# Attention: narrow products in column and row tiles, and the decay's bias added by VectorE

## The chip, the core and the metric

The kernel runs on 1 core of one Trainium2 chip. The metric is the device time of one execution in microseconds (us), lower is better. Times shown are of whole executions; the profile is of one of them.

## What is computed

A layer of two halves. The first is an RWKV-6 attention over x of shape (2, 4096, 512), behind a layer norm with a learned shift and scale; the second a feed-forward part with 4-bit block quantization. The change touches the attention alone. Cut to what matters there:

```
sx  = shift(x) - x
xxx = x + sx * time_maa_x
m   = tanh(xxx @ tm_w1).reshape(B, T, 5, 32)          # tm_w1: 512 x 160
mix = time_maa_wkvrg + einsum('btfa,fac->btfc', m, tm_w2)
xw, xk, xv, xr, xg = [x + sx * mix[:, :, i] for i in range(5)]
r, k, v, g = xr @ Wr, xk @ Wk, xv @ Wv, silu(xg @ Wg)
ww  = time_decay + tanh(xw @ td_w1) @ td_w2           # td_w1: 512 x 64, td_w2: 64 x 512
w   = exp(-exp(ww))
# per head, over time: y_t = r_t (state + u k_t v_t'); state = w_t * state + k_t v_t'
out = groupnorm(y) * g @ Wo
```

## The kernel before

Tokens go in 32 blocks of 128 per sequence, both sequences (B = 2) together, so that a block has BT = 256 columns; channels lie on the 128 partitions in G = 4 groups. `attention` writes each engine's order out by hand: `pe_body`, `act_body`, `dve_body`, `pool_body` and `sp_body` are called for i = 0 to 33 and work in one pass on three blocks. Block i is mixed and projected (`do_p`), block i - 1 goes through the recurrence (`do_w`), block i - 2 through the output product (`do_f`). Most passes run in a hardware loop of three laps with nine passes written out in each. Engines meet at semaphores, one `Signal` each; `after(engine, signal, block, k)` is a wait.

In a pass TensorE first does eight steps of 32 tokens for the recurrence: `pe_scores` (L404, L408, L410, L415, matmuls in 32x32 tiles) and `pe_y` (L430, L433, likewise). Between the steps stand the two halves of `pe_g` (L509), `pe_td1` (L474), the five mixing products `pe_delta` (L462), two output products `pe_wo` (L522, 512 columns) and `pe_td2` (L482). Then come the k, r and v projections `pe_proj` (L495), with `pe_x` (L442, transposes of the next block) and `pe_tm1` (L450) among them.

The places that the change touches:

- `pe_tm1` multiplies `xxx` by `tm_w1`: its first 128 columns give mixings 0 to 3, with one 128x128 stationary tile per channel group; its last 32 give mixing 4, with a 128x32 tile and all 256 token columns. Both write to `SMALL`, one PSUM bank.
- `act_m` (L575 to L578) takes the tanh of both, once as fp32 and once rounded to fp32r; `dve_m` (L752, L753) forms the rest, the difference of the two.
- `act_stack` (L588) copies, for each mixing, the 32 rows of value or rest into four partition groups of `m_stack`, 20 copies a block. `act_affine` (L604) follows on ScalarE; VectorE's `dve_z` (L918) waits for it.
- `pe_td1` multiplies the mixed `xf` by `td_w1` into 64 rows of `SMALL`; ScalarE's tanh (L671) writes `u1`, whose 65th row holds ones. `pe_td2` multiplies by `w_td2`, whose 65th row is the decay bias, into the two banks `PROJ`. `dve_ww` (L774) takes the minimum with 80 into `wexp`, and ScalarE's two exponentials (L616, L619) follow.
- VectorE's steps are `dve_A` (L865, L872, L878, L894), one per recurrence step, and `dve_mix` (L762), one per mixing. A mixing waits for its product and frees `PROJ` for the next.

Of the kernel before, what the change touches and what calls it, by code (L numbers as in the profile page):

```python
# [30 lines left out]
ALU = mybir.AluOpType  # L31
ACT = mybir.ActivationFunctionType
AX_X = mybir.AxisListType.X

HEADS = [slice(r, r + 32) for r in range(0, 128, 32)]
E_MAX = 1e30

P = 128
B, T, C = 2, 4096, 512
H, K = 16, 32  # L40
G = C // P
HG = P // K
A_RANK, D_RANK = 32, 64
NMIX = 5
TC = 128
NI = T // TC
BT = B * TC
Q = TC // 32
NX = G * B * Q
EPS = 1e-5  # L50
# [40 lines left out]
def after(eng, signal, chunk, k=None):  # L91

    value = signal.at(chunk, k)
    if not isinstance(value, int) or value > 0:
        eng.wait_ge(signal.sem, value)
# [40 lines left out]
def attention(nc, x1, x, maa_x, maa, tm_w1, tm_w2, decay, td_w1, td_w2, faaaa, Wr, Wk, Wv, Wg, Wo,  # L136
              ln_w, ln_b, c_in, wmod, ident_in, diag_in, pick_in, ni=NI):
    with ExitStack() as ctx:
        ctx.enter_context(nc.allow_non_contiguous_dma(reason="per-channel columns, a few hundred bytes each"))

        def sb(name, shape, dt=F32):
            return ctx.enter_context(nc.sbuf_tensor(name, shape, dt))
# [14 lines left out]
        w_tm1 = sb("w_tm1", [P, G, NMIX * A_RANK])  # L157
        w_tm2 = sb("w_tm2", [P, NMIX, C], F32R)
        w_td1 = sb("w_td1", [P, G, D_RANK])
        w_td2 = sb("w_td2", [D_RANK + 1, C])  # L160

        col_maax, col_u = sb("col_maax", [P, G]), sb("col_u", [P, G])
        col_maa = sb("col_maa", [P, NMIX, G])
        col_sa, col_ca = sb("col_sa", [P, G, B]), sb("col_ca", [P, G, B])
        col_lnw, col_lnb = sb("col_lnw", [P, G]), sb("col_lnb", [P, G])
# [13 lines left out]
        m_full = xxx[:, 0:2].rearrange("p g b t -> p g (b t)")  # L179
        m_hi = xxx[:, 2:4].rearrange("p g b t -> p g (b t)")  # L180
        m_part = (m_hi.bitcast(F32R), m_full.bitcast(F32R))
        u1 = sb("u1", [D_RANK + 1, BT])
        rT = sb("rT", [P, G, B, TC])
        kvar = sb("kvar", [P, 4, G, B, TC])
        rcol = sb("rcol", [P, NX, SEND])
# [39 lines left out]
        with nc.Block() as blk:  # L225
            @blk.sync
            def _(sp):
                def load(dst, src):
                    sp.dma_start(dst, src).then_inc(loaded, 16)
                    n_loads[0] += 1  # L230
                sp.dma_start(kvar[:, 0:2].rearrange("p a g b t -> p (a g b t)").rearrange("p (g n) -> p g n", g=G),
                             wmod[:, 0:C].rearrange("(g p) n -> p g n", p=P)).then_inc(mod_loaded, 16)
                sp.dma_start(kvar[:, 2:4].rearrange("p a g b t -> p (a g b t)").rearrange("p (g n) -> p g n", g=G),
                             wmod[:, C:2 * C].rearrange("(g p) n -> p g n", p=P)).then_inc(mod_loaded, 16)
                sp.dma_start(rcol_flat[:, 0:G * C].rearrange("p (g n) -> p g n", g=G),
                             wmod[:, 2 * C:3 * C].rearrange("(g p) n -> p g n", p=P)).then_inc(mod_loaded, 16)
                for g in range(G):
                    sp.dma_start(c_t[:, g, :], c_in[:, g * P:(g + 1) * P].rearrange("b p -> p b")).then_inc(mod_loaded, 16)
                for dst, src in ((w_r[:], Wr), (w_k[:], Wk), (w_v[:], Wv), (w_g[:], Wg), (w_o_raw, Wo), (w_tm1[:], tm_w1), (w_td1[:], td_w1)):
                    load(dst, src.rearrange("(g p) n -> p g n", p=P))  # L240
                for part in range(4):
                    load(w_full[A_RANK * part:A_RANK * (part + 1)], tm_w2.rearrange("f a n -> a f n"))
                load(w_td2[0:D_RANK, :], td_w2)
                load(ident[:], ident_in)
                load(diag[:], diag_in)
                load(pick_f, pick_in)
                load(col_maax[:], maa_x.rearrange("(g p) -> p g", p=P))
                load(w_td2[D_RANK:D_RANK + 1, :], decay.unsqueeze(0))
                load(col_u[:], faaaa.rearrange("(g h) k -> (h k) g", g=G))
                for f in range(NMIX):  # L250
                    load(col_maa[:, f, :], maa[f].rearrange("(g p) -> p g", p=P))
                load(col_lnw[:], ln_w.rearrange("(g p) -> p g", p=P))
                load(col_lnb[:], ln_b.rearrange("(g p) -> p g", p=P))
                sp.wait_ge(loaded, 16 * n_loads[0])

            @blk.gpsimd
            def _(pool):
                nc.gpsimd.memset(neg_half[:], -0.5)
                nc.gpsimd.memset(state[:], 0.0)
                nc.gpsimd.memset(u1[:], 1.0)  # L260
                nc.gpsimd.memset(F4[:], 1.0)
                nc.gpsimd.memset(G4[:], 1.0).then_inc(zeroed, 1)

# [181 lines left out]
        def pe_tm1(pe, i):  # L445
            after(pe, xxx_done, i)
            after(pe, hT_done, i)
            for lo, hi, o in ((0, P, 0), (P, NMIX * A_RANK, BT)):
                for k in range(G):
                    last = nc.tensor.matmul(SMALL[0:hi - lo, o:o + BT], w_tm1[:, k, lo:hi],  # L450
                                            xxx[:, k].rearrange("p b t -> p (b t)"), start=(k == 0), stop=(k == G - 1))
            last.then_inc(tm1_done.sem, 1)

        def pe_delta(pe, i, j):
# [14 lines left out]
        def pe_td1(pe, i):  # L469
            xf_wait(pe, i, 0)  # L470
            after(pe, mf_done, i)
            after(pe, gu_done, i - 1)
            for k in range(G):
                last = nc.tensor.matmul(SMALL[0:D_RANK, 0:BT], w_td1[:, k, :], xf[:, 0, k].rearrange("p b t -> p (b t)"),  # L474
                                        start=(k == 0), stop=(k == G - 1))
            last.then_inc(td1_done.sem, 1)

        def pe_td2(pe, i):
            after(pe, u1_done, i)
            after(pe, mixed, i)  # L480
            for g in range(G):
                last = nc.tensor.matmul(PROJ[g // 2][:, (g % 2) * BT:(g % 2 + 1) * BT], w_td2[:, g * P:(g + 1) * P], u1[:],  # L482
                                        start=True, stop=True)
            last.then_inc(td2_done.sem, 1)

        def pe_proj(pe, i, j, free, halves=(0, 1)):
# [86 lines left out]
        def act_m(act, i):  # L573
            after(act, tm1_done, i)
            nc.scalar.activation(m_full[:, 0], SMALL[:, 0:BT], ACT.Tanh)  # L575
            nc.scalar.activation(m_full[0:A_RANK, 1], SMALL[0:A_RANK, BT:2 * BT], ACT.Tanh)
            nc.scalar.activation(m_part[0][:, 0], SMALL[:, 0:BT], ACT.Tanh)
            nc.scalar.activation(m_part[0][0:A_RANK, 1], SMALL[0:A_RANK, BT:2 * BT], ACT.Tanh).then_inc(mf_done.sem, 1)  # L578

        def act_stack(act, i):  # L580
            after(act, mf_done, i)
            after(act, m_done, i)
            after(act, delta_done, i - 1)
            for j in range(NMIX):
                f = ORDER[j]
                src = slice(A_RANK * (f % 4), A_RANK * (f % 4 + 1))
                for part in range(4):
                    last = nc.scalar.activation(m_stack[A_RANK * part:A_RANK * (part + 1), j, :], m_part[part % 2][src, f // 4, :], ACT.Copy)  # L588
                last.then_inc(m_stacked.sem, 1)

        def act_yT(act, c, b):
# [71 lines left out]
        def act_body(act, i, do_p, do_w, do_f, more, more2):  # L663
            c, f = i - 1, i - 2
            if do_w:
                act_gu(act, c, 0)
                act_gu(act, c, 1)
            if do_p:
                after(act, td1_done, i)
                after(act, td2_done, c)  # L670
                nc.scalar.activation(u1[0:D_RANK, :], SMALL[0:D_RANK, 0:BT], ACT.Tanh).then_inc(u1_done.sem, 1)  # L671
            if more:
                act_xn(act, i + 1)
            if do_w:
                act_yT(act, c, 0)
            if do_p:
                act_w(act, i)
            if do_p:
                act_fg(act, i)
                act_k(act, i, 0)  # L680
            if do_w:
                act_yT(act, c, 1)
            if more:
                act_hT(act, i + 1)
            if do_w:
                act_square(act, c)
            if do_p:
                act_k(act, i, 1)
                act_r(act, i, 0)
                act_r(act, i, 1)  # L690
                act_k32(act, i)
                act_m1(act, i)
            if more:
                act_m(act, i + 1)
            if more:
                act_stack(act, i + 1)
            if do_w:
                act_affine(act, c)
# [51 lines left out]
        def dve_m(dve, i):  # L750
            after(dve, mf_done, i)
            nc.vector.tensor_tensor(m_part[1][:, 0], m_full[:, 0], m_hi[:, 0], ALU.subtract)  # L752
            nc.vector.tensor_tensor(m_part[1][0:A_RANK, 1], m_full[0:A_RANK, 1], m_hi[0:A_RANK, 1], ALU.subtract).then_inc(m_done.sem, 1)  # L753

        def dve_mix(dve, i, j):
            after(dve, delta_done, i, j + 1)
# [13 lines left out]
        def dve_ww(dve, i):  # L770

            after(dve, td2_done, i)
            after(dve, m_stacked, i)
            nc.vector.tensor_scalar(flat4(wexp), banks[:, 2:4].rearrange("p s n -> p (s n)"), 80.0, None, ALU.min).then_inc(ww_done.sem, 1)  # L774

        def dve_der_w(dve, i):

# [922 lines left out]
```

## Time and profile before

| | us |
|---|---|
| median of 3 runs | 4545.55 |
| lowest and highest | 4528.36 and 4548.22 |
| the profiled execution | 4564.24 |
| its span, first to last instruction | 4562.4 |
| TensorE busy in it | 3895.7 (85%) |
| VectorE busy | 3591.5 (79%) |
| ScalarE busy | 1506.1 (33%) |
| GpSimd busy | 1182.1 (26%) |

PE is TensorE's matmuls and PEld its weight loads, which overlap; DVE is VectorE, ACT ScalarE, POOL GpSimd. A fp32 matmul shows as two records, a fp32r one as one. "Issue" is idle time in which an engine waited for nothing that the profile shows. L numbers are lines of the kernel before.

### The profile page before, as it was taken

What the parts mean: (1) busy time and instruction counts of PE and PEld (TensorE: products, weight loads), DVE (VectorE), ACT (ScalarE), POOL (GpSimd) and SP (SyncE); (2) the same over time, 40 slices, a digit from 0 to 9 for tenths busy, and PEclk for the clock granted to TensorE, in tenths of its full rate; (3) what the DMA queues carried; (4) which work ended last, traced back from release to release, by engine and by line L of the source; (5) the groups of instructions that cost most, each with busy time, mean ns of one, the idle gap of its engine ahead of it and who ended that gap; (6) DMA issues with size and microseconds to landing.
All of it is one profiled execution on the core that took longest, in us unless ns stands there. A gap on an engine that the chain in (4) does not pass through costs nothing. (4 is left out here: it accounts for less than half of the span.)

```text
span 4562.4 us, 152511 instructions
## 1 busy us (share of the span) xinstructions
PE 3895.7 (85%) x64712; PEld 2623.4 (57%) x64712; DVE 3591.5 (79%) x7929; ACT 1506.1 (33%) x2683; POOL 1182.1 (26%) x736
## 2 busy tenths in 40 slices
PE   4889888888988888898898942499999999999998
PEld 3767676666766766777676721244444444444444
DVE  4777877867776776777787739789999999999997
ACT  2434343343433433434342302233333232323232
POOL 1121211112111121212212104433333333333332
PEclk7999998989999999999998965699999999999999
DMA  3000000000000000000000020000101111010100
GB/s 106 12 27 21 22 26 19 29 17 22 26 22 22 21 22 26 22 26 17 26 21 17 21 92 28 14 29 29 36 28 36 31 33 34 30 36 29 36 28 29
DMA packets 72983, 133.01 MB, mean 29 GB/s; under 512 B 12705, under 2 KB 13473, under 8 KB 72290
## 3 DMA queue, kind: packets, MB, share of 16 engines
q1 hardware_dynamic: 72290, 123.00, 8.5%
q8 instruction: 528, 8.65, 0.8%
q14 instruction: 165, 1.35, 0.1%
HBM read 89.43 MB, written 33.55 MB: 27 GB/s over the span
## 5 line engine op out<-in xcount | busy, mean ns | idle before, releaser
L712 POOL TENSOR_TENSOR xf<-xf,hT 128x1024 f32<-128x1024 f32 x128 | 309.3, 2417 | 1209.1 <-DVE xf L762 1209.1
L878 DVE COPY_PREDICATED Am<-pick,banks 128x64 f32<-128x64 uint8 (+2 forms) x1792 | 460.5, 257 | 125.4 <-DVE Am L878 8.6
L1580 PE MATMUL fbank<-gT,xqT 128*128 128x464 f16 (+1 forms) x2304 | 492.0, 364 | 61.6 <-ACT xqT L1503 60.0
L1602 PE MATMUL fbank<-dT,hqT 128*128 128x512 f16 x2112 | 488.4, 380 | 50.7 <-ACT hqT L1513 50.7
L1580 PE MATMUL fbank<-uT,xqT 128*128 128x464 f16 (+1 forms) x2304 | 488.2, 362 | 2.1 <-issue 2.1
L1527 ACT ACTIVATE sil<-fbank,und 128x464 f32<-128x464 f32 (+1 forms) x192 | 125.1, 652 | 860.4 <-PE fbank L1580 860.4
L723 POOL TENSOR_TENSOR yrs<-yvar,neg_half 128x32 f32<-128x32 f32 x32 | 174.0, 5437 | 896.3 <-DVE yvar L907 896.3
L1580 PEld LDWEIGHTS fbank<-gT,xqT 128*128 128x128 f16 x2304 | 221.2, 98 | 313.0 <-issue 84.6
L1580 PEld LDWEIGHTS fbank<-uT,xqT 128*128 128x128 f16 x2304 | 225.3, 98 | 234.8 <-issue 5.5
L1602 PEld LDWEIGHTS fbank<-dT,hqT 128*128 128x128 f16 x2112 | 196.9, 98 | 266.1 <-issue 33.4
L762 DVE SCALAR_TENSOR_TENSOR xf<-banks,col_maa,sx 128x256 f32<-128x256 f32 x640 | 265.2, 477 | 94.8 <-PE banks L462 94.3
L522 PE MATMUL banks<-w_o,yn 128*128 128x512 f32 x512 | 293.6, 727 | 19.8 <-DVE yn L918 15.9
L1385 POOL TENSOR_TENSOR hq<-q16h,s16h 128x1408 f16<-128x1408 f16 x64 | 163.7, 2558 | 523.9 <-DVE hq L1338 523.9
L588 ACT ACTIVATE m_stack<-xxx 32x256 fp32r<-32x256 f32 x640 | 264.9, 414 | 75.9 <-DVE xxx L753 58.9
L509 PE MATMUL banks<-xf,w_g 128*128 128x256 f32 x1024 | 260.9, 411 | 7.3 <-issue 4.0
L430 PE MATMUL banks<-Am,v_s 32*32 32x32 f32 x8192 | 192.6, 198 | 85.1 <-issue 79.2
L865 DVE TENSOR_TENSOR Am<-banks,diag 128x128 f32<-128x128 f32 x256 | 72.5, 283 | 238.7 <-PE banks L415 233.7
L495 PE MATMUL banks<-xf,w_k 128*128 128x256 f32 x1024 | 249.2, 398 | 7.5 <-issue 6.1
L433 PE MATMUL banks<-r,state 32*32 32x32 f32 x8192 | 192.3, 196 | 52.1 <-issue 52.1
L430 PEld LDWEIGHTS banks<-Am,v_s 32*32 32x32 f32 x8192 | 160.5, 108 | 127.9 <-issue 123.0
L495 PE MATMUL banks<-xf,w_v 128*128 128x256 f32 x1024 | 229.5, 382 | 0.0
L509 PEld LDWEIGHTS banks<-xf,w_g 128*128 128x128 f32 x1024 | 204.5, 205 | 41.8 <-issue 5.7
(233 smaller groups left out, 8417.5 us busy)
## 6 DMA issues: line engine op xcount, KB each, us to landing
x_tok<-in_L_attn_x SPq DMA_DIRECT2D x32, 512.0 KB, 4.0
xres<-in_L_attn_x SPq DMA_DIRECT2D x32, 512.0 KB, 3.6
x_after_attention<-xres SPq DMA_DIRECT2D x32, 512.0 KB, 3.7
xl<-x_after_attention SPq DMA_DIRECT2D x64, 256.0 KB, 2.8
xr<-x_after_attention SPq DMA_DIRECT2D x64, 256.0 KB, 2.8
out<-xr SPq DMA_DIRECT2D x64, 256.0 KB, 2.1
raw_g<-in_L_wmod SPq DMA_DIRECT2D x3, 1024.0 KB, 5.1
raw_g<-in_L_ffn_w_gate SPq DMA_DIRECT2D x1, 2816.0 KB, 11.4
```

What stands on the lines that cost most here:

```text
L430: nc.tensor.matmul(out, v_s[d, g, b, q, :], Am[d, n % 2, g, :], start=True, stop=False)
L433: last = nc.tensor.matmul(out, state[d, b, q, g, :], r32[d, X, :], start=False, stop=True)
L495: last = nc.tensor.matmul(PROJ[h][:, (g % 2) * BT:(g % 2 + 1) * BT], w[:, k, g * P:(g + 1) * P], buf[:, k].rearrange("p b t -> p (b t)"), ...
L509: last = nc.tensor.matmul(SMALL[:, (g % 2) * BT:(g % 2 + 1) * BT], w_g[:, k, g * P:(g + 1) * P], xf[:, NMIX - 1, k].rearrange("p b t -> p ...
L522: last = nc.tensor.matmul(SMALL[:], yn[:, k, b, :], w_o[:, b, k, :], start=(k == 0), stop=(k == G - 1))
L588: last = nc.scalar.activation(m_stack[A_RANK * part:A_RANK * (part + 1), j, :], m_part[part % 2][src, f // 4, :], ACT.Copy)
L712: nc.gpsimd.tensor_tensor(xf[:, j % NXF].rearrange("p g b t -> p (g b) t"), xf[:, j % NXF].rearrange("p g b t -> p (g b) t"), hT[:, :, :, ...
L723: nc.gpsimd.tensor_tensor(yrs[:], yvar[:], neg_half[:], ALU.pow).then_inc(yrs_done.sem, 1)
L762: last = nc.vector.scalar_tensor_tensor(xf[:, j % NXF, g], PROJ[g // 2][:, (g % 2) * BT:(g % 2 + 1) * BT].rearrange("p (b t) -> p b t", b= ...
L878: nc.vector.copy_predicated(dst, mask, src).then_inc((done or A_step).sem, 1)
L1580: last = nc.tensor.matmul(GU[2 * pair + t][:, 0:w], xqT[:, u, a, g, :], W[:, b_, g, lo_:hi_], start=(k == 0), stop=(k == 3 * G - 1))
L1602: last = nc.tensor.matmul(DN[1 - u][:], hqT[:, a, kk, :], dT[:, b_, kk, :], start=(k == 0), stop=(k == 3 * KF - 1))
```

## The change

Three things change in the attention.

The last 32 columns of `tm_w1`: the 256 token columns are cut in four runs of QT = 64, and each run goes to its own column tile (32 stationary columns, output on partitions 0, 32, 64, 96). So the result lies as 128 rows of 64 columns, not as 32 rows of 256. Tanh and difference run on that shape, and the copies for mixing 4 bring each run back to its columns: sixteen copies of 64 columns instead of four of 256.

The decay's first product runs as two column tiles of 64, one per sequence; its second as two row tiles, each with its own half of `u1`, its own copy of `w_td2` and its own bank. `PROJ[b]` now holds one sequence; before, each bank held two channel groups of both.

The bias row and the row of ones go. The bias is loaded as the column `col_decay`, and VectorE adds it in `dve_ww`, in four instructions, one for each channel group. The memset of `u1` goes, `td_w2` is loaded twice.

```
-        w_td2 = sb("w_td2", [D_RANK + 1, C])
+        w_td2 = sb("w_td2", [P, C])
+        col_decay = sb("col_decay", [P, G])
-        u1 = sb("u1", [D_RANK + 1, BT])
+        u1 = sb("u1", [P, TC])
...
-                load(w_td2[0:D_RANK, :], td_w2)
+                for b in range(B):
+                    load(w_td2[HALVES[b], :], td_w2)
-                load(w_td2[D_RANK:D_RANK + 1, :], decay.unsqueeze(0))
+                load(col_decay[:], decay.rearrange("(g p) -> p g", p=P))
...
-                nc.gpsimd.memset(u1[:], 1.0)
...
-            for lo, hi, o in ((0, P, 0), (P, NMIX * A_RANK, BT)):
-                for k in range(G):
-                    last = nc.tensor.matmul(SMALL[0:hi - lo, o:o + BT], w_tm1[:, k, lo:hi],
-                                            xxx[:, k].rearrange("p b t -> p (b t)"), start=(k == 0), stop=(k == G - 1))
+            for k in range(G):
+                nc.tensor.matmul(SMALL[:, 0:BT], w_tm1[:, k, 0:P], xxx[:, k].rearrange("p b t -> p (b t)"), start=(k == 0), stop=(k == G - 1))
+            for k in range(G):
+                for d, rows in enumerate(HEADS):
+                    last = nc.tensor.matmul(SMALL[rows, BT:BT + QT], w_tm1[:, k, P:P + A_RANK], xxx[:, k].rearrange("p b t -> p (b t)")[:, QT * d:QT * (d + 1)],
+                                            start=(k == 0), stop=(k == G - 1))
...
             for k in range(G):
-                last = nc.tensor.matmul(SMALL[0:D_RANK, 0:BT], w_td1[:, k, :], xf[:, 0, k].rearrange("p b t -> p (b t)"),
-                                        start=(k == 0), stop=(k == G - 1))
+                for b in range(B):
+                    last = nc.tensor.matmul(SMALL[HALVES[b], 0:TC], w_td1[:, k, :], xf[:, 0, k, b], start=(k == 0), stop=(k == G - 1))
...
-            after(pe, u1_done, i)
-            after(pe, mixed, i)
+            settled_after(pe, mod_done, (u1_done, i), (mixed, i))
             for g in range(G):
-                last = nc.tensor.matmul(PROJ[g // 2][:, (g % 2) * BT:(g % 2 + 1) * BT], w_td2[:, g * P:(g + 1) * P], u1[:],
-                                        start=True, stop=True)
+                for b in range(B):
+                    last = nc.tensor.matmul(PROJ[b][:, g * TC:(g + 1) * TC], w_td2[HALVES[b], g * P:(g + 1) * P], u1[HALVES[b]], start=True, stop=True)
...
-            nc.scalar.activation(m_full[0:A_RANK, 1], SMALL[0:A_RANK, BT:2 * BT], ACT.Tanh)
+            nc.scalar.activation(m_full[:, 1, 0:QT], SMALL[:, BT:BT + QT], ACT.Tanh)
...
-                    last = nc.scalar.activation(m_stack[A_RANK * part:A_RANK * (part + 1), j, :], m_part[part % 2][src, f // 4, :], ACT.Copy)
+                    rows = HEADS[part]
+                    if f < 4:
+                        last = nc.scalar.activation(m_stack[rows, j, :], m_part[part % 2][HEADS[f], 0, :], ACT.Copy)
+                    else:
+                        for d in range(4):
+                            last = nc.scalar.activation(m_stack[rows, j, QT * d:QT * (d + 1)], m_part[part % 2][HEADS[d], 1, 0:QT], ACT.Copy)
...
-                nc.scalar.activation(u1[0:D_RANK, :], SMALL[0:D_RANK, 0:BT], ACT.Tanh).then_inc(u1_done.sem, 1)
+                nc.scalar.activation(u1[:], SMALL[:, 0:TC], ACT.Tanh).then_inc(u1_done.sem, 1)
...
-            nc.vector.tensor_tensor(m_part[1][0:A_RANK, 1], m_full[0:A_RANK, 1], m_hi[0:A_RANK, 1], ALU.subtract).then_inc(m_done.sem, 1)
+            nc.vector.tensor_tensor(m_part[1][:, 1, 0:QT], m_full[:, 1, 0:QT], m_hi[:, 1, 0:QT], ALU.subtract).then_inc(m_done.sem, 1)
...
-            nc.vector.tensor_scalar(flat4(wexp), banks[:, 2:4].rearrange("p s n -> p (s n)"), 80.0, None, ALU.min).then_inc(ww_done.sem, 1)
+            for g in range(G):
+                last = nc.vector.tensor_scalar(wexp[:, g], banks[:, 2:4, g * TC:(g + 1) * TC], col_decay[:, g:g + 1], 80.0, ALU.add, ALU.min)
+            last.then_inc(ww_done.sem, 1)
```

`HEADS` are the four runs of 32 partitions, `HALVES` the two of 64.

TensorE's order of the first pass, around the three products (each row: line, operation, output and inputs, output's shape, count of matmuls). Before:

```order
L450 MATMUL banks<-xxx,w_tm 128x256 x4
L450 MATMUL banks<-xxx,w_tm 32x256 x4
L462 MATMUL banks<-m_stack,w_tm 128x256 x8
L474 MATMUL banks<-xf,w_td 64x256 x4
L462 MATMUL banks<-m_stack,w_tm 128x256 x12
L482 MATMUL banks<-u,w_td 128x256 x4
```

With the change:

```order
L451 MATMUL banks<-xxx,w_tm 128x256 x4
L454 MATMUL banks<-xxx,w_tm 32x64 x16
L466 MATMUL banks<-m_stack,w_tm 128x256 x8
L479 MATMUL banks<-xf,w_td 64x128 x8
L466 MATMUL banks<-m_stack,w_tm 128x256 x12
L486 MATMUL banks<-u,w_td 128x128 x8
```

Nothing has changed places; 12 matmuls a block have become 32, and each streams fewer columns.

ScalarE's order from the tanh of the mixings to the gate's, with the change:

```order
L578 ACTIVATE xxx<-banks 128x256
L579 ACTIVATE xxx<-banks 128x64
L580 ACTIVATE xxx<-banks 128x256
L581 ACTIVATE xxx<-banks 128x64
L592 ACTIVATE m_stack<-xxx 32x256 x16
L595 ACTIVATE m_stack<-xxx 32x64 x16
```

Before, the last two rows were one, twenty copies of 32x256.

## Rows read from the trace of the kernel before

**Rows 1.** The page: span and busy shares.
```profile
span 4562.4 us, 152511 instructions
...
PE 3895.7 (85%) x64712; PEld 2623.4 (57%) x64712; DVE 3591.5 (79%) x7929; ACT 1506.1 (33%) x2683; POOL 1182.1 (26%) x736
```

**Rows 2.** Windows: us, then busy (count) of PE, PEld, DVE, ACT, POOL, granted clock, DMA.
```profile
500.00:1000.00 500.00, 444.44 (x10567) 349.68 (x10567) 376.91 (x936) 187.93 (x398) 97.22 (x43) 0.92 0.08 24
```

**Rows 3.** Waits of PE, 100 to 2600 us: waiting, releaser: total, times, longest.
```profile
PE banks L430 <- issue: 77.0, 50, 2.5
...
PE banks L415 <- DVE kT L852: 23.1, 31, 0.7
```

**Rows 4.** Waits of DVE, 100 to 2600 us.
```profile
DVE Am L865 <- PE banks L415: 205.0, 68, 6.3
...
DVE xf L762 <- PE banks L462: 88.7, 66, 4.2
DVE xxx L774 <- PE banks L482: 35.8, 21, 3.9
```

**Rows 5.** Groups of PE, 100 to 2600 us: form xrecords | busy, mean ns | idle before.
```profile
L482 PE MATMUL banks<-u,w_td 65*128 65x256 f32 x252 | 106.3, 594 | 2.7 <-DVE xf L762 2.7
L474 PE MATMUL banks<-xf,w_td 128*64 128x256 f32 x248 | 68.8, 427 | 0.0
L450 PE MATMUL banks<-xxx,w_tm 128*32 128x256 f32 x248 | 59.3, 382 | 0.0
```

**Rows 6.** Timeline of PE: start, length, line, records, idle before.
```profile
1199.78 3.37 PE L474 MATMUL banks<-xf,w_td 128*64 128x256 f32 x8
...
1210.13 0.76 PE L404 MATMUL banks<-rcol,kvar 32*32 32x80 f32 x32
...
1210.80 0.23 PE L410 MATMUL banks<-rcol,kvar 32*32 32x16 f32 x8
...
1212.72 0.22 PE L430 MATMUL banks<-Am,v_s 32*32 32x32 f32 x3 [0.65 <-issue]
...
1216.12 0.20 PE L410 MATMUL banks<-rcol,kvar 32*32 32x16 f32 x1 [1.01 <-issue]
```

**Rows 7.** Timeline of PE later: tm1 and a second td1.
```profile
1245.78 3.73 PE L450 MATMUL banks<-xxx,w_tm 128*128 128x256 f32 x16
...
1278.41 1.94 PE L474 MATMUL banks<-xf,w_td 128*64 128x256 f32 x8
```

**Rows 8.** DMA queues, 100 to 2600 us: packets, MB, share.
```profile
q8 instruction: 429, 7.03, 1.2%
```

**Rows 9.** Windows: a stretch and the one right after it.
```profile
1195.90:1199.30 3.40, 1.67 (x159) 1.53 (x148) 3.26 (x9) 0.00 (x0) 2.09 (x1) 1.00 0.02 5
1199.30:1202.70 3.40, 3.29 (x23) 1.97 (x24) 2.46 (x12) 0.00 (x0) 0.98 (x3) 0.50 0.03 7
```

**Rows 10.** Timeline of ACT in one block.
```profile
1250.36 0.36 ACT L578 ACTIVATE xxx<-banks 32x256 fp32r<-32x256 f32 x1
1252.88 8.55 ACT L588 ACTIVATE m_stack<-xxx 32x256 fp32r<-32x256 f32 x20 [2.15 <-DVE xxx L753]
1261.45 2.07 ACT L604 ACTIVATE yn<-yn,col_lnb,col_lnw 128x256 f32<-128x256 f32 x4
```

**Rows 11.** Timeline of DVE in one block.
```profile
1229.54 0.29 DVE L865 TENSOR_TENSOR Am<-banks,diag 128x128 f32<-128x128 f32 x1 [4.77 <-PE banks L415]
...
1266.11 1.25 DVE L918 TENSOR_TENSOR yn<-yn,gate 128x1024 f32<-128x1024 f32 x1
1269.68 1.66 DVE L762 SCALAR_TENSOR_TENSOR xf<-banks,col_maa,sx 128x256 f32<-128x256 f32 x4 [2.33 <-PE banks L462]
```

**Rows 12.** Groups of ACT, 100 to 2600 us.
```profile
L616 ACT ACTIVATE xxx<-xxx 128x1024 f32<-128x1024 f32 x32 | 33.8, 1056 | 574.4 <-DVE xxx L774 574.4
...
L564 ACT ACTIVATE hT<-hT 128x8 f32<-128x8 f32 x31 | 6.7, 217 | 1.9 <-PE banks L442 0.4
```

**Rows 13.** Timeline of DVE in the set-up.
```profile
42.63 0.21 DVE L285 CAST pick<-yT 128x112 uint8<-128x112 f32 x1
```

More of the change, by code:

```diff
@@ L47 @@
 BT = B * TC
+QT = BT // 4
+HALVES = [slice(0, 64), slice(64, 128)]
 Q = TC // 32
@@ L159, in attention @@
         w_td1 = sb("w_td1", [P, G, D_RANK])
-        w_td2 = sb("w_td2", [D_RANK + 1, C])
-        col_maax, col_u = sb("col_maax", [P, G]), sb("col_u", [P, G])
+        w_td2 = sb("w_td2", [P, C])
+        col_maax, col_u, col_decay = sb("col_maax", [P, G]), sb("col_u", [P, G]), sb("col_decay", [P, G])
         col_maa = sb("col_maa", [P, NMIX, G])
@@ L575, in act_m @@
             nc.scalar.activation(m_full[:, 0], SMALL[:, 0:BT], ACT.Tanh)
-            nc.scalar.activation(m_full[0:A_RANK, 1], SMALL[0:A_RANK, BT:2 * BT], ACT.Tanh)
+            nc.scalar.activation(m_full[:, 1, 0:QT], SMALL[:, BT:BT + QT], ACT.Tanh)
             nc.scalar.activation(m_part[0][:, 0], SMALL[:, 0:BT], ACT.Tanh)
-            nc.scalar.activation(m_part[0][0:A_RANK, 1], SMALL[0:A_RANK, BT:2 * BT], ACT.Tanh).then_inc(mf_done.sem, 1)
+            nc.scalar.activation(m_part[0][:, 1, 0:QT], SMALL[:, BT:BT + QT], ACT.Tanh).then_inc(mf_done.sem, 1)
         def act_stack(act, i):
@@ L585, in act_stack @@
                 f = ORDER[j]
-                src = slice(A_RANK * (f % 4), A_RANK * (f % 4 + 1))
                 for part in range(4):
-                    last = nc.scalar.activation(m_stack[A_RANK * part:A_RANK * (part + 1), j, :], m_part[part % 2][src, f // 4, :], ACT.Copy)
+                    rows = HEADS[part]
[4 more added lines that the diff above has]
+                            last = nc.scalar.activation(m_stack[rows, j, QT * d:QT * (d + 1)], m_part[part % 2][HEADS[d], 1, 0:QT], ACT.Copy)
                 last.then_inc(m_stacked.sem, 1)
```

## The prediction

> **What bounds the kernel now.** Read the busy shares first [rows 1]: no engine is at its limit over the whole span. The change touches the attention stage alone, some 2,500 us of it, so I go to windows inside it [rows 2]: TensorE is busy 444.44 of 500 us, VectorE 376.91, ScalarE 187.93, at a granted clock of 0.92. Then the waits. TensorE hardly waits for anyone: for VectorE's transpose of k 23.1 us in all [rows 3]. Its other idle time is "issue", the largest entry 77.0 us in 50 places, though the program holds no wait there. VectorE does wait, and for TensorE: 205.0 us for scores, 88.7 for the mixing's products, 35.8 for the decay's [rows 4]. So the end of this stage is set by TensorE's own chain: its matmuls, its issue stalls, and its clock. ScalarE and VectorE matter where their slack is small.
>
> The decay's first product ran 248 records, 8 per block of tokens, so 31 blocks in 2,500 us: 80.6 us a block [rows 5]. The sum is made per block and multiplied by 32.
>
> **TensorE's matmuls.** All three products are fp32, each matmul two records. td2 takes 106.3 us over 252 records, 3.37 a block; td1 68.8 over 248, 2.22; tm1's narrow half 59.3 over 248, 1.91 [rows 5]. tm1's sixteen records take 3.73 us [rows 7], its narrow half, with 32 stationary columns, 1.91 of it: array columns left idle cost full time. After the change td1 and td2 stream 128 columns per matmul in two tiles, tm1's rest 64 in four. Do tiles run side by side? 32 records of 80 columns in 32x32 tiles take 0.76 us [rows 6]; at the pace of a 256-column record (3.73 us for 16, 0.23 each [rows 7]) one by one they would take 32 x 0.073 = 2.3 us. So tiles that share neither rows nor columns overlap fourfold, less the last one's drain. Tiles that share rows (td1, tm1) are not in the trace. Bounds: no gain, or the full factor. I take the full factor, since the 32x32 rows are the nearest. td2 halves, -1.69; td1 halves, -1.11; tm1's rest goes to a quarter, -1.43. Together -4.23 us a block.
>
> A rule speaks against tm1's part, whose factor is taken from the moving columns. The Trainium skill, TensorEngine Tiling (Array Packing), section Performance Considerations, gives each matmul an overhead of about 60 cycles and warns against dividing a dimension that is already small. At 2.4 GHz an estimate by it is 25 ns x 32 records = 0.8 us where I have 0.48, some 10 us less gain in all. The trace disagrees: eight 16-column records end within 0.23 us [rows 6].
>
> **Instruction supply.** 429 instruction packets of 16 KB fed TensorE in this stretch [rows 8], 13.8 a block, about 250 instructions each. The stalls at 1212.72 and 1216.12 lie 3.40 us apart, and the records from the one to the other are 45, 4 for a mixing product and 78 for scores: 127 pairs of load and matmul, one packet [rows 6]. A packet of small matmuls is used up in about 2.4 us, yet the next comes only after 3.40. So a packet costs at least 3.4 us, and time saved inside a packet that takes less is lost. tm1 lies among 96 long projection records and td2 beside the output product: both keep their saving. td1 is surrounded by small tiles. With it at 1.94 us [rows 7] a packet holding it takes about 3.9, and after the saving 2.8, so 0.6 comes back as stall; at half clock (3.37 us [rows 6]) nothing does. I charge 0.55, with bounds 0 and 1.1. Besides, 20 more matmuls in the program are 80 instructions a block, 0.31 packet. TensorE's idle is 0.111 of 80.6 us, 9.0, less 0.75 for the transpose, over 13.8 packets 0.60 each: +0.19.
>
> **Clock.** Between 1195.9 and 1199.3 TensorE was busy 1.67 of 3.4 us, and the next stretch ran at 0.50, the 1.2 GHz level, although busy 3.29 of 3.40 [rows 9]. So low clock follows a stretch with little matmul work. The clock of 0.92 means some 13 us of low time a block. The change takes long work out of the small-tile stages, and I expect more such stretches. Each costs between 0 (small work follows) and 1.7 us (long work follows at half pace; td1 shows 3.37 against 1.94). I take one more every second block, +0.85, bounds 0 and 3.4 (two a block).
>
> **ScalarE.** For the last of the five mixings, four copies of 256 columns become sixteen of 64. Length by columns: 1,056 ns for 1,024, 217 for 8 [rows 12], 414 for 256 (20 in 8.55 us without overlap, [rows 10]), so about 0.20 us fixed and 0.84 ns a column: 0.25 for 64, 0.27 with the step. 16 x 0.27 less 4 x 0.43 is +2.6 us before the affine step; the shorter tanh and subtraction give back some 0.3. That lies on a path: the affine ends at 1263.52 and VectorE's gating product starts at 1266.11 [rows 10, 11], 2.6 of slack. tm1's saving moves VectorE 1.4 earlier, but the copies start hardly earlier, since they wait 2.15 us for VectorE's subtraction. The product is then late by up to 2.3 - 1.2 = 1.1. The next mixing waited 2.33 for TensorE in this block [rows 11], which hides it; where it doesn't wait, it counts. I charge 0.3, bounds 0 and 1.1.
>
> **VectorE.** ww becomes four instructions; the nearest row has four of 256 columns in 1.66 us [rows 11] where one took about 1.23, so 0 to +0.43. It is free: after it VectorE sat idle 4.77 us for the next scores [rows 11], behind the output product. Without that cover it would be 0.43. In the scores loop VectorE waits for TensorE at the scores and at 66 mixings only, of 155 [rows 4]; elsewhere it is itself the later one, and TensorE's saving is not passed on. I charge 0.6 of td1's and td2's, bounds 0 and 1.2.
>
> **Edits at no cost.** The second copy of the decay weights (128 KB) and the bias column hide behind VectorE's set-up, which reaches its first loaded operand at 42.63 with no idle before it [rows 13]. The dropped memset is on idle GpSimd. td2's waits are the same two, plus one long since met.
>
> **Sum.** -4.23 + 0.55 + 0.19 + 0.85 + 0.3 + 0.6 = -1.74 us a block, -56 in 32. Profiled execution: 4564.2 - 56 = 4508. The median of the runs, 4545.55, stands 18.7 below it, so I predict 4490 as a median.
>
> **Rivals.**
> 1. *Column tiles don't overlap*, as they share all rows: tm1 and td1 save nothing. Left are -1.69 + 0.19 + 0.4 (clock) + 0.3 = -0.8 a block, -26: about 4520. For: no row shows such tiles. Against: the 32x32 rows. Chance 0.12.
> 2. *Supply and clock take it all*: all of td1 lost, three more half-clock stretches every two blocks (2.55): -4.23 + 1.1 + 0.19 + 2.55 + 0.3 = -0.1, no change, 4540. For: issue stalls and low clock stand together in rows 6 and 9. The Trainium skill, TensorE: Matmul & The Clock Gate, section on why this matters, warns of throughput drops after idle gaps; rows 9 agree. Against: 2.8 us less of 46 is little. Chance 0.10.
> 3. *Slower: ScalarE's copies.* If 64 columns cost as much as 256 (0.43 a step), the copies grow by 5.2, the gating product comes 2.3 later than now, all of tm1's gain goes, and -4.23 + 1.43 + 2.3 + 0.55 + 0.19 + 0.85 = +1.1 a block, +35: 4580. It decides once a copy takes over 0.36. For: partition-shifted copies are only seen at 256. Against: the 8-column row of 217 ns. Chance 0.06.
> 4. *The tiles do nothing*, td2's included: about 4550. Chance 0.02.
>
> **How the numbers follow.** The forecast has 0.70: its own range, by the bounds, 4455 to 4520. With rivals 1 and part of 2 the range is 4455 to 4538. A measurement here tells about 0.5% (23 us) from no change. Faster: 0.70 and half of rival 1, 0.76. Same: the other half, rival 2, rival 4, 0.18. Slower 0.06.
>
> **What would show it.** td2's busy time near 53 us, td1's near 36, tm1's rest near 16; VectorE's wait for td2 (35.8) almost gone; more issue idle and a granted clock one or two hundredths lower in windows of this stage; copies of 64 columns near 0.25 us; the gating product waiting for the affine. Wrong if the copies take 0.4, if tm1's rest stays near 1.9 us a block, or if the clock falls below 0.89.

## The result, and the profile after

| | before | after |
|---|---|---|
| median of 4 runs each, us | 4545.99 | 4484.56 |
| lowest and highest | 4528.36, 4548.22 | 4470.44, 4490.96 |
| profiled execution | 4564.24 | 4490.96 |

The ratio is 0.9869, interval 0.9841 to 0.9897: faster by 1.3%. The forecast was 4490. The page of the kernel after, to set beside [rows 1]:

```profile
span 4488.8 us, 155551 instructions
...
PE 3793.4 (85%) x65992; PEld 2593.9 (58%) x65992; DVE 3589.2 (80%) x8025; ACT 1568.8 (35%) x3067; POOL 1181.0 (26%) x735
```

TensorE is busy 102 us less. How many of these the clock on the wall gets is best read from an instruction that comes once a block. VectorE's transpose of k, kernel before (durations in ns, then first and last start in us):

```profile
L852 DVE STREAM_TRANSPOSE kT<-kvar x32: 1201/1203/1204, 131.1 to 2622.5; 128x1024 f32<-128x1024 f32 x32
```

and after:

```profile
L861 DVE STREAM_TRANSPOSE kT<-kvar x32: 1201/1202/1204, 125.1 to 2558.5; 128x1024 f32<-128x1024 f32 x32
```

Over 31 intervals that is 80.37 us a block before and 78.50 after: -1.87, where the sum said -1.74. Of the 73 us between the two profiled executions 58 lie in these intervals, 6 ahead of the first transpose, 10 behind the last. By the windows of this stretch TensorE's busy time a block goes from 71.5 to 68.6 us, its idle time from 8.9 to 9.9. From here on "a block" means this spacing, and 2400 us of a window hold 2400 / 80.37 = 29.9 blocks before and 30.6 after.

The three products, groups of PE after, 100 to 2500 us (form, records, busy us, mean ns, idle before), beside [rows 5]:

```profile
L486 PE MATMUL banks<-u,w_td 64*128 64x128 f32 x480 | 55.7, 396 | 9.4 <-issue 6.7 <-DVE xf L769 2.7
L479 PE MATMUL banks<-xf,w_td 128*64 128x128 f32 x480 | 36.8, 293 | 8.9 <-issue 8.9
...
L454 PE MATMUL banks<-xxx,w_tm 128*32 128x64 f32 x992 | 20.3, 222 | 0.0
```

With 16, 16 and 32 records a block these are 1.86, 1.23 and 0.65 us, against 3.37, 2.22 and 1.91: -3.76 together. So tiles that share all their rows do run side by side. The mixing's product as a whole, timeline of PE, took 3.73 us [rows 7] and takes 2.5 now:

```profile
1210.58 1.89 PE L451 MATMUL banks<-xxx,w_tm 128*128 128x256 f32 x8
1212.39 0.65 PE L454 MATMUL banks<-xxx,w_tm 128*32 128x64 f32 x32
```

td1 is not always left whole. Here its sixteen records, 1.4 us in all, are cut by a stall that is longer than they are:

```profile
1240.46 0.43 PE L479 MATMUL banks<-xf,w_td 128*64 128x128 f32 x3
1242.68 0.93 PE L479 MATMUL banks<-xf,w_td 128*64 128x128 f32 x13 [1.79 <-issue]
```

Waits of PE after, 100 to 2500 us (total, times, longest), beside [rows 3]:

```profile
PE banks L432 <- issue: 62.7, 38, 3.3
...
PE banks L417 <- DVE kT L861: 23.1, 31, 0.7
...
PE banks L512 <- ACT gu L668: 12.5, 13, 1.7
PE banks L479 <- issue: 8.9, 6, 1.8
```

The issue entries of this view add up to 260.9 us in 197 places; before, in the same window, 230.3 in 170. Per block 7.71 became 8.53, +0.82. TensorE's wait for ScalarE at the gate's projection, 3.1 us before, is 12.5.

Waits of DVE after, 100 to 2500 us, beside [rows 4]:

```profile
DVE Am L874 <- PE banks L417: 189.2, 76, 5.3
DVE v_s L856 <- PE banks L498: 69.7, 31, 2.3
DVE xf L769 <- PE banks L466: 67.6, 65, 3.1
DVE yn L927 <- ACT yn L611: 24.7, 28, 1.7
...
DVE xxx L782 <- PE banks L486: 3.8, 6, 1.7
```

The wait for td2 (35.8) is all but gone. A new one is there: the gating product L927 waits for ScalarE's affine in 28 blocks, 0.8 us a block. Why, shows the timeline of ACT in one block:

```profile
1213.87 0.25 ACT L579 ACTIVATE xxx<-banks 128x64 f32<-128x64 f32 x1
...
1217.48 6.84 ACT L592 ACTIVATE m_stack<-xxx 32x256 fp32r<-32x256 f32 x16 [2.98 <-DVE xxx L760]
1224.34 4.23 ACT L595 ACTIVATE m_stack<-xxx 32x64 fp32r<-32x64 f32 x16
1228.60 2.08 ACT L611 ACTIVATE yn<-yn,col_lnb,col_lnw 128x256 f32<-128x256 f32 x4
1232.03 0.60 ACT L667 ACTIVATE gate<-banks 128x512 f32<-128x512 f32 x1 [1.35 <-DVE yn L927]
```

The copies take 11.1 us where they took 8.55 [rows 10], the affine ends that much later, the product with it, and the gate's eviction L667, which overwrites what the product reads, waits for the product. That is how TensorE comes to its 12.5 us. One row of windows, beside [rows 2], shows the clock, 0.91 for 0.92 (over 100 to 2500 us it is 0.93 in both kernels):

```profile
500.00:1000.00 500.00, 437.96 (x11127) 353.56 (x11129) 386.63 (x972) 209.26 (x500) 101.42 (x43) 0.91 0.07 22
```

### The profile page after: what moved, and what is told of

Read it like the earlier page. It is cut to its first block and busy times, and to the rows that moved or that the text cites. A ratio compares the mean times of both kernels' runs of the same rounds, so it can differ in the third digit from the quotient of the medians.

```text
span 4488.8 us, 155551 instructions
## 1 busy us (share of the span) xinstructions
PE 3793.4 (85%) x65992; PEld 2593.9 (58%) x65992; DVE 3589.2 (80%) x8025; ACT 1568.8 (35%) x3067; POOL 1181.0 (26%) x735
## 5 line engine op out<-in xcount | busy, mean ns | idle before, releaser
L512 PE MATMUL banks<-xf,w_g 128*128 128x256 f32 x1024 | 261.8, 413 | 14.1 <-ACT gu L668 12.5
L592 ACT ACTIVATE m_stack<-xxx 32x256 fp32r<-32x256 f32 x512 | 211.9, 414 | 99.6 <-DVE xxx L760 81.2
L623 ACT ACTIVATE xxx<-xxx 128x1024 f32<-128x1024 f32 x32 | 33.8, 1057 | 566.3 <-DVE xxx L782 566.3
```

What stands on the lines that cost most here:

```text
L512: last = nc.tensor.matmul(SMALL[:, (g % 2) * BT:(g % 2 + 1) * BT], w_g[:, k, g * P:(g + 1) * P], xf[:, NMIX - 1, k].rearrange("p b t -> p ...
L592: last = nc.scalar.activation(m_stack[rows, j, :], m_part[part % 2][HEADS[f], 0, :], ACT.Copy)
```

## The experiments

**How to read the ratios.** The runs came in three sets of four kernels, on chips where the kernel before took 4575.25, 4564.36 and 4551.42 us. So each kernel is told by its ratio to the kernel before on its own chip, with its 95% interval. 1% is 1.4 us a block. The change itself was timed only in the comparison above, against 4545.99 us, so where it is set beside one of these kernels, the two ratios come from different chips. And each kernel's trace is of one execution: a small difference between two traces is a hint and not a measurement.

### Each part alone

The first kernel is the kernel before with the mixing's narrow part of the change, its tanh, difference and copies; all else is as before.

```
+            for k in range(G):
+                for d, rows in enumerate(HEADS):
+                    last = nc.tensor.matmul(SMALL[rows, BT:BT + QT], w_tm1[:, k, P:P + A_RANK], ...[:, QT * d:QT * (d + 1)], ...)
```

> Only the narrow half of tm1 is tiled, with its sixteen copies; td1, td2 and the bias as before. Theory (ScalarE takes most of it): in the changed kernel's trace the place of tm1 shrank from 3.73 to 2.47 us, 1.26 a block, but the gating product waits 24.7 us in 30 blocks, 0.8 a block, for the affine behind the copies: net 0.3 to 0.6 a block, 10 to 20 us faster. Rival (the copies are hidden by mixing's waits for TensorE): all of 1.26 x 32, 40 us faster. Second rival (column tiles only pay together with the others): no change.

Measured 4514.14 us, ratio 0.9873 (0.9850 to 0.9896), 58 us faster, beyond even the rival's 40. That is 1.8 us a block (1.5 to 2.1 by the interval), more than the 1.26 that the product itself got shorter, although the price of the copies is paid in full. Waits of DVE, 100 to 2500 us:

```profile
DVE yn L926 <- ACT yn L612: 22.4, 27, 1.6
...
DVE xxx L782 <- PE banks L486: 14.0, 7, 3.9
```

The wait for the unchanged td2 fell from 31.2 us in this window to 14.0: a product that didn't change is waited for less. Something else had moved; what, this run doesn't tell.

The second has td1 as column tiles only; two tanh instead of one write both halves back to the old `u1`.

```
+                for b in range(B):
+                    last = nc.tensor.matmul(SMALL[HALVES[b], 0:TC], w_td1[:, k, :], xf[:, 0, k, b], ...)
```

> Only td1 runs in two column tiles; ScalarE brings the two halves back with two tanh. Theory (instruction supply takes half of what td1 saves): TensorE's place of td1 shrinks by 1.0 us a block, the issue idle in the scores steps near it grows by 0.3 to 0.6, so 10 to 20 us faster. Rival (supply takes nothing): 32 to 35 us faster. Rival (supply takes all): within 5 us of before.

Measured 4603.19, ratio 1.0067 (1.0040 to 1.0093): **slower**, by about 1 us a block, though td1 itself is 1 us shorter. All three expectations had it faster or the same. Group, wait and window of this kernel, 100 to 2500 us:

```profile
L477 PE MATMUL banks<-xf,w_td 128*64 128x128 f32 x464 | 37.1, 303 | 7.6 <-issue 7.6
```

```profile
PE banks L432 <- issue: 69.6, 35, 3.5
PE banks L435 <- issue: 68.5, 38, 2.5
```

```profile
100.00:2500.00 2400.00, 2103.24 (x50713) 1662.60 (x50713) 1738.82 (x4415) 876.24 (x1864) 459.86 (x202) 0.90 0.07 22
```

Its issue entries add up to 268.1 us in 29.3 blocks (82.0 us each), 9.2 a block, where the kernel before has 7.7 and the kernel with the bias alone, below, on the same chip, 8.1 (237.5 in 29.5 blocks): as much as td1 could save, or more. The granted clock is 0.90; those two have 0.93 and 0.92.

The third has td2 as row tiles with the bias on VectorE, and two tanh that fill the two halves of `u1`; the fourth has the bias alone.

```
+            for g in range(G):
+                last = nc.vector.tensor_scalar(wexp[:, g], PROJ[...], col_decay[:, g:g + 1], 80.0, ALU.add, ALU.min)
```

> td2 runs in two row tiles with its bias added by VectorE; td1 and tm1 as before, two tanh for u1. Theory (td2's saving passes whole, since VectorE waits for scores behind the output product right after it): 1.4 to 1.6 us a block, 45 to 50 us faster, the largest of the three parts. Rival (the wait moves to VectorE, whose chain of scores and mixings ends only then): 1.0 a block, about 30 us faster, and VectorE's wait before its next scores step grows instead of shrinking.

> Only the bias is moved: 64 rows in td2 without tiles, column added by VectorE in four instructions, no memset. Theory (hidden behind the output product): within 5 us of before, while the four instructions take 1.66 us in place of 1.23. Rival (they lie on the path): 0.43 x 32, 14 us slower.

Row tiles with the bias: 4508.52, ratio 0.9865 (0.9841 to 0.9888), 62 us faster where I had 45 to 50. The bias alone: 4584.18, ratio 1.0028 (1.0010 to 1.0046), 0.4 us a block, 13 us in all, which is the rival's price and not the theory's. So the four instructions, 1.66 us where one took 1.23, are not quite free. Against the bias alone the row tiles bring 1.6%, 2.3 us a block, for a product that got 1.6 us shorter (3.50 to 1.89). The granted clock over 100 to 2500 us is 0.94 in the one trace and 0.92 in the other; whether the rest of the gain came with it was not tested.

### Does the count of instructions cost?

20 small matmuls (80 instructions, as many as the change adds) into the kernel before, ahead of its wait for the transpose of k, on operands that are ready; what they write is overwritten. The same with 16 in the kernel with td1 alone.

```
             if n == 0:
+                for e in range(20):
+                    d = HEADS[e % 4]
+                    nc.tensor.matmul(scm[d, ...], kvar[d, 2, g, b, 32 * q:32 * q + 32], rcol[d, X, X0:SEND], start=True, stop=True)
```

> The kernel before with 20 more small matmuls a block: repeats of one 16-column score product, same values to the same place, put where TensorE waits 0.75 us for the transpose of k anyway. They bring as many instructions a block (80) as the change does and, hidden in that wait, no work on the path. Theory (where the packets of instructions begin within a block matters): the time moves by 15 us or more, either way, with TensorE's issue stalls standing at other places than before. Rival (only the amount of work matters): within 8 us of before.

> td1 alone in column tiles, which was 28 us slower than before, and now 16 of the same hidden small matmuls, so that the block has as many instructions as in the changed kernel. Theory (the loss of td1 alone came from the packets' places): 20 us or more faster than td1 alone. Rival (td1's saving is lost whatever the places, through stalls and a lower clock): the same as td1 alone within 10 us, ratio near 1.006.

Measured 4578.99, ratio 1.0052 (1.0026 to 1.0079), 0.7 us a block; and 4590.90, ratio 1.0060 (1.0038 to 1.0083), the same as td1 alone. So 80 more instructions cost 0.7 us where they hardly take room, above the 0.19 that I had charged; 64 more on top of td1 cost nothing that shows. How the 0.7 comes about is open. In the trace with 20 more TensorE's issue idle is 0.6 us a block above the kernel before (8.3 for 7.7), but its whole idle time is the same within 0.1 (9.0 for 8.9), since its waits for others are shorter; its busy time is 0.7 longer (72.2 for 71.5), of which the added products are some 0.3, and the granted clock is 0.91 for 0.93. The loss of td1 alone did not go away when its packets were shifted by 64 instructions; other shifts were not run.

### ScalarE's order

The affine is put ahead of the last mixing's copies, in the change and in the kernel before.

```
-                act_stack(act, i + 1)
+                act_stack(act, i + 1, range(NMIX - 1))
...
                 act_affine(act, c)
+            if more:
+                act_stack(act, i + 1, range(NMIX - 1, NMIX))
```

> The changed kernel with ScalarE's affine step moved ahead of the sixteen copies for the last mixing, which are needed only some 30 us later. Theory (the copies delay the gating product by 0.8 us a block): VectorE's wait for the affine (24.7 us) goes, 0.4 to 0.8 us a block, ratio 0.981 to 0.984 against 0.987 of the change. Rival (that wait only takes the place of the mixing's wait for TensorE): the wait goes, but the ratio stays 0.987.

> The same move of the affine step in the kernel before, where the gating product never waited for it. Both theories: within 8 us of before. It is the control for the run before this one, since here the instructions of TensorE are untouched: a change beyond 8 us would say that the time depends on small shifts that this study doesn't follow.

The change with it: 4478.21, ratio 0.9828 (0.9791 to 0.9864), the fastest kernel of all, though its interval overlaps that of the change. The kernel before with it: 4553.06, ratio 0.9974 (0.9950 to 0.9997), 11 us faster. That control was expected within 8 us, since no product waited for the affine there. So a move of this kind may bring 0.3% with no wait to remove, and the 0.4% in the change can't be put down to the affine on this evidence. Timelines of the change so ordered, first ACT, then DVE, in the block shown above:

```profile
1216.93 6.84 ACT L593 ACTIVATE m_stack<-xxx 32x256 fp32r<-32x256 f32 x16 [2.97 <-DVE xxx L763]
1223.91 2.08 ACT L612 ACTIVATE yn<-yn,col_lnb,col_lnw 128x256 f32<-128x256 f32 x4
```

```profile
1229.26 1.24 DVE L930 TENSOR_TENSOR yn<-yn,gate 128x1024 f32<-128x1024 f32 x1
```

The affine ends 9.1 us after the first copy begins (1216.93 to 1225.99) where it ended 13.2 after (1217.48 to 1230.68). The product no longer waits, and TensorE's wait at the gate's projection is 2.0 us where it was 12.5. The rival is right in part all the same. The next mixing now waits longer for TensorE:

```profile
DVE xf L772 <- PE banks L466: 86.8, 69, 3.9
```

That is 2.8 us a block where it was 2.2 (67.6 in the window), so of the 0.8 that VectorE no longer waits for the affine it waits 0.6 here.

### Leaving out one part

The change without td1's tiles, should the second experiment have shown td1 to be a loss, and the same with the affine moved; then the change without the mixing's part.

```
-                for b in range(B):
-                    last = nc.tensor.matmul(SMALL[HALVES[b], 0:TC], w_td1[:, k, :], xf[:, 0, k, b], ...)
+                last = nc.tensor.matmul(SMALL[0:D_RANK, 0:BT], w_td1[:, k, :], xf[:, 0, k].rearrange("p b t -> p (b t)"), ...)
```

> The changed kernel with td1 as it was before (one product of 256 columns), tm1 and td2 tiled. Theory (td1's tiles are a loss in company too, as alone: what they save comes back as issue stall and as half-clock time of the output product): faster than the change by about the 0.7% that td1 alone lost, ratio 0.978 to 0.983. Rival (the parts overlap, and td1's loss alone was of its own surroundings): ratio 0.987 to 0.993, the change or worse.

> The run before this one with the affine step moved ahead of the last mixing's copies. Theory: both gains add, ratio 0.974 to 0.979, the fastest of all. Rival (one takes the place of the other): 0.982 to 0.984, as with the moved affine alone.

> The changed kernel with tm1, its tanh and its copies as before: td1 and td2 alone. If parts add as they measured alone (td1 +0.7%, td2 -1.35%), ratio 0.993. If tm1's gain in company is only what its own place saves less the wait for the affine (0.4 a block, 15 us), then ratio 0.990. If tm1 gives nothing in company: 0.987.

| in the kernel | ratio to before | interval |
|---|---|---|
| tm1 | 0.9873 | 0.9850 to 0.9896 |
| td1 | 1.0067 | 1.0040 to 1.0093 |
| td2 and bias | 0.9865 | 0.9841 to 0.9888 |
| td1, td2 and bias | 0.9958 | 0.9940 to 0.9976 |
| tm1, td2 and bias | 1.0003 | 0.9983 to 1.0024 |
| the same, affine moved | 0.9914 | 0.9886 to 0.9941 |
| all (the change) | 0.9869 | 0.9841 to 0.9897 |

The change without td1's tiles took 4546.44 us, with the affine moved 4505.11, and without the mixing's part 4529.78. My expectation for the kernel without td1 fell, and the rival with it (0.987 to 0.993), as did both for the same with the affine moved (0.974 to 0.979, and 0.982 to 0.984). Two parts that each bring 1.3% bring nothing together, and td1, a loss by itself, brings 1.3% on top of them, if the change's ratio, from another chip, may be set beside theirs. Besides the tiles, the kernel without td1 has two tanh for `u1` where the change has one. td1 with td2 is near the product of the two (0.9931). The odd one is tm1 with td2: 2.6% short of 0.9740, 3.7 us a block.

Its trace shows something. Timeline of PE in five successive blocks, the rows that follow a stall in the first step's y products, between the output product and the k projection (and 1206.62, a stall in the last step before it):

```profile
1138.80 0.22 PE L435 MATMUL banks<-r,state 32*32 32x32 f32 x2 [1.99 <-issue]
...
1206.62 0.26 PE L432 MATMUL banks<-Am,v_s 32*32 32x32 f32 x2 [2.05 <-issue]
...
1217.80 0.26 PE L435 MATMUL banks<-r,state 32*32 32x32 f32 x6 [2.20 <-issue]
1218.02 3.69 PE L498 MATMUL banks<-xf,w_k 128*128 128x256 f32 x16
...
1297.83 0.18 PE L432 MATMUL banks<-Am,v_s 32*32 32x32 f32 x1 [1.80 <-issue]
...
1378.04 0.23 PE L432 MATMUL banks<-Am,v_s 32*32 32x32 f32 x3 [2.15 <-issue]
...
1458.03 0.18 PE L435 MATMUL banks<-r,state 32*32 32x32 f32 x1 [1.44 <-issue]
```

1138.8, 1217.8, 1297.8, 1378.0, 1458.0: one stall in each block at the same place, and, in the block shown with it, another some 11 us before. Over 100 to 2500 us a stall of more than 1 us stands in y products between td2 and the k projection in 24 of 29 blocks. In the kernel before it is 11 of 30, with td2 and the bias alone 12 of 30, in the change 9 of 30, and with tm1 alone 0 of 30. What recurs there for some blocks is a stall among the third step's scores:

```profile
1242.24 0.30 PE L410 MATMUL banks<-rcol,kvar 32*32 32x48 f32 x3 [2.14 <-issue]
...
1321.42 0.23 PE L410 MATMUL banks<-rcol,kvar 32*32 32x48 f32 x1 [1.78 <-issue]
...
1401.61 0.24 PE L412 MATMUL banks<-rcol,kvar 32*32 32x16 f32 x3 [2.03 <-issue]
```

Waits of PE in the kernel with tm1 and td2, 100 to 2500 us:

```profile
PE banks L432 <- issue: 88.3, 47, 2.5
PE banks L435 <- issue: 71.3, 37, 2.4
PE banks L406 <- issue: 35.4, 37, 3.7
...
PE banks L512 <- ACT gu L668: 25.5, 23, 1.6
```

Its issue entries add up to 269.8 us, 9.0 a block, against 7.4 with tm1 alone (225.8) and 7.9 with td2 alone (241.5); the wait at the gate's projection is 25.5 us against 1.8 and 2.9; and the matmuls around the stalls are slower, the k projection 415 ns a record against 384 and 398.

Packets are the likely reason for the fixed places. The instruction queue's packets in the window, times the block (from the same transposes), over 2400 us, give packets per block: 412 and 80.37 before, 13.80; 425 and 78.89 with tm1, 13.97; 421 and 80.26 with tm1 and td2, 14.08; 423 and 78.51 with td2, 13.84; 433 and 78.50 after, 14.16. My reading, not shown, is this: near a whole number the packets end at the same instructions in block after block, and a stall that starts out in a cheap or a dear place stays there; otherwise the places drift and the price averages out. The recurring places are shown. That they make up the missing 2.6% is argued: no run shifted the packets of the kernel with tm1 and td2 and left its work alone. Nor does the count alone decide. The kernel before with 20 more matmuls has 14.03 packets (415 and 81.14) and lost only 0.5%, with a stall at that place in 12 of 29 blocks.

Moving the affine brought this kernel 0.9% on the same chip (4505.11 for 4546.44), so up to 1.3 us of its block went by ScalarE's queue (the control above gained 0.3% by the same move): TensorE's wait at the gate's projection fell from 25.5 to 6.1 us. That the delay costs most here, where TensorE waits for it in 23 places, is part of the odd loss. With the affine moved the stall at that place is still there in 25 of 30 blocks, at 14.05 packets (424 and 79.54), and the kernel is still 1.7% short of 0.9740. What that rest is, and why td1's tiles end it, stays open. tm1 with td1 was not run.

### Twice the 16-column scores

In the change each score product of 16 columns is issued twice, 512 more instructions a block.

```
+                for d in HEADS:
+                    nc.tensor.matmul(scm[d, ...], kvar[d, 2, ...], rcol[d, X, X0:SEND], start=True, stop=True)
```

> The changed kernel with each 16-column score product issued twice, to the same place: 128 more small matmuls a block, 512 instructions, two packets, and by the 8 ns a record of such products 2.0 us of TensorE's time a block. Theory (in the scores steps a packet costs at least 3.4 us): 4 to 7 us a block, 130 to 220 us more than the change, ratio 1.015 to 1.035, and issue idle up by a quarter or more. Rival (only their own time counts): 2.0 x 32, 64 us, ratio 1.001.

Measured 4745.38, ratio 1.0434 (1.0395 to 1.0473), beyond even the supply theory's range. Against the change's ratio that is 5.7%, 8.0 us a block. Group, wait and window of this kernel, 100 to 2500 us:

```profile
L414 PE MATMUL banks<-rcol,kvar 32*32 32x16 f32 x7072 | 217.4, 183 | 25.6 <-issue 25.5
```

```profile
PE banks L419 <- issue: 73.1, 43, 4.0
```

```profile
100.00:2500.00 2400.00, 2056.58 (x56181) 1673.25 (x56182) 1641.66 (x4280) 886.17 (x2093) 434.18 (x193) 0.88 0.07 21
```

The packets per block are 16.19 (446 and 87.13), 2.03 more than in the change, so each brought 4.0 us with it, where I had read at least 3.4 from two stalls [rows 6]. The matmuls themselves are small: seven such records start within 0.07 us of each other in the timelines, some 2 us for all 256. So 512 instructions cost four times what their products take. Not all of that is waiting for packets. By the two traces the block is 8.6 us longer: TensorE's issue idle is 3.4 us more (11.9 for 8.5), its whole idle time 2.5 more, its busy time 6.1 more (74.7 for 68.6), of which 2 are the added products. The other 4 came at a granted clock of 0.88 for 0.93, with the gate's projection at 442 ns a record for 414 and td1 at 371 for 293. Stalls and the lower clock came together, and no run tells them apart.

## Why the prediction was right, step by step

**The three products.** td2 -1.51 us (predicted -1.69), td1 -0.99 (-1.11), tm1's narrow half -1.26 (-1.43). The size from the 32x32 rows was right within 12%, always on the hopeful side. Those rows have 0.76 us for 2.3 one by one, threefold, and the forecast took the full factor of four for tm1; the runs show 1.91 to 0.65, threefold again, and 1.8-fold for td1 and td2. The rule of the Trainium skill that I had weighed, TensorEngine Tiling (Array Packing), section Performance Considerations, would make the narrow half 0.8 us; I had 0.48, the trace has 0.65, between them.

**Supply.** Charged 0.55 and 0.19, together 0.74; the issue idle grew by 0.82. The size held for the whole change. It was not right part by part: 1.1 to 1.5 us for td1 alone, where I charged 0.55 and allowed 1.1 at most, and 0.7 for 80 hidden instructions, busy time and stalls together, where I charged 0.19 for stalls. The reason named, that time saved between small tiles comes back as stalls, fits td1 alone, whose issue idle grew by as much as td1 saved; the rest of its loss is busy time: TensorE's is 71.9 us a block, 0.4 above the kernel before though td1 took 0.9 less, at the lower clock of 0.90.

**Clock.** Charged 0.85 by one more low stretch in every second block. That step failed for the change: the clock over 100 to 2500 us is 0.93 in both kernels. In its place other matmuls got a little longer, 235 to 238 ns for the 80-column scores (256 records within 6.4 us), 411 to 414 for the gate's projection, 321 to 329 for the mixings. Each group's busy time scaled by its mean, these and their like come to some 0.6 us a block, most of it in the small tiles; what lengthened them no run tells. With td1 alone the clock did fall, to 0.90.

**ScalarE.** 64 columns take 254 ns (I had 250), the sixteen copies 4.23 us, so the copies grew by 2.5 us (2.6). But the delay was charged at 0.3, and more hangs on it: VectorE waits 0.8 us a block for the affine, and the wait is handed on to TensorE by way of the gate's eviction, which I had not followed. Moving the affine brought 0.4% by the two ratios in the change and 0.9% in the kernel without td1's tiles, 0.6 and 1.3 us a block, against 0.26% in the kernel before, where there was no wait to remove. So the delay's price is shown for the kernel without td1's tiles, some 0.6% or 0.9 us a block, and not for the change.

**VectorE and the edits at no cost.** The wait for td2 went as foreseen. The bias was put at nothing with up to 0.43 without cover; alone it costs 0.4 us. The step that failed is the cover: it was read from one block, where VectorE then sat idle 4.77 us, and ScalarE's exponentials stand behind the same four instructions in every block. That they are the path is a guess that no run tests. The 0.6 for VectorE's own chain could not be separated.

**The sum.** -3.76 in the three products, +0.82 supply, +0.6 longer matmuls and +0.2 more waits of TensorE for other engines make -2.1, and the blocks show -1.87. TensorE's busy and idle time as a whole give the -1.87, by -2.90 and +1.03; where the 0.3 between the two accounts lies was not traced. So the total of -1.74 came out well, 4490 for 4484.56. That was luck in part. The savings were taken 0.47 too high and the clock 0.85 too dear, the longer matmuls (0.6) were not foreseen, and the bias and ScalarE's delay were taken too low. The profiled execution was forecast at 4508 and took 4490.96, 17 us less: 16 of the 73 us saved there lie outside the blocks' intervals, and the 18.7 by which the median stood below the profiled execution before are 6.4 after. Nor is the range of 4455 to 4520 what the stated bounds add up to, which is -4.04 to +2.76 us a block with the tiles at their full factor, 4416 to 4634; how it was narrowed isn't said. The parts do not add, either: alone they give 2.0% in sum, together 1.3%, and the pair of the two good ones gives nothing. A sum of terms could not have told that pair.

**The rivals.** That column tiles don't overlap is refuted by 2.22 us a block becoming 1.23 and 1.91 becoming 0.65. That supply and clock take it all is refuted for the change, but it is what happened to td1 alone: more issue idle and a clock of 0.90. The copies at 0.43 us each, the slower case, are refuted by 254 ns.

## What to carry to other kernels

Where an engine's idle time is issue, count instructions and packets beside busy time: tried alone, products shortened among long matmuls kept their saving and more, and one among small tiles gave it all back. Follow a delay on a lightly used engine to the buffer that it holds: a lateness of 2.5 us on an engine 35% busy reached TensorE by a tile that had to be read first, and a change of order took that wait away. Run such a change of order in the kernel where nothing waits, too: here it gained 0.3% even so. And don't drop a part because it loses by itself, or keep one because it wins: time the combination.

## What the runs showed that I had not expected

- Two parts with ratios 0.9873 and 0.9865 give 1.0003 together, and a third with 1.0067 alone brings them to 0.9869.
- A wait of TensorE's for instructions recurs at one place, 79 to 80 us apart, in 24 of 29 blocks of a kernel of 14.08 packets a block; with tm1 alone it is there in none.
- 512 more instructions in small tiles cost 8.0 us a block, 4.0 us for each packet, in stalls and in matmuls at a lower clock, for some 2 us of products.
- 80 instructions whose work lies beside a wait cost 0.5% of the whole kernel.
- ScalarE's affine moved ahead in the kernel before, where nothing waited for it, gained 0.3%.
